# One unrolled pipeline through all heads of the first two attentions, key-major values for two groups, the block quantisation at other steps, and SiLU as one ScalarE function

## The reference

```python
x = x + tanh(g_xattn[i]) * attention_i(layernorm(x), ctx)
x = x + tanh(g_ffn[i])   * ffn_i(layernorm(x))
```

```python
q = latents @ Wq; k, v = hidden_states @ Wk, hidden_states @ Wv   # hidden_states = context, then latents
out = softmax(q k^T * scale) v                                    # 8 (or 4) heads share one k and one v
return out @ Wo
```

## Time and profile before

| | us |
|---|---|
| median of 3 runs | 1492.81 (1490.13 to 1494.4) |
| the profiled execution: its own time | 1491.04 |
| its span, first to last instruction | 1489.3 |
| PE busy | 1369.5 (92%) |
| DVE busy | 965.4 (65%) |
| ACT busy | 599.4 (40%) |
| POOL busy | 467.3 (31%) |
| attention 0, about | 44 to 654 |
| attention 1, about | 729 to 1062 |
| network of layer 2, about | 1284 to 1398 |
| network of layer 3, about | 1417 to 1487 |

### The profile page before, as it was taken

The page is one execution under the profiler, slowest core; times in us unless marked ns, Lnnn a source line. Parts: engine busy times, 40 slices in busy tenths (PEclk is TensorE's granted clock), DMA queues, the critical chain, the costliest instruction groups (busy, mean ns, idle before and its releaser), DMA issues.

```text
span 1489.3 us, 22423 instructions
## 1 busy us (share of the span) xinstructions
PE 1369.5 (92%) x8021; PEld 1073.0 (72%) x8027; DVE 965.4 (65%) x1394; ACT 599.4 (40%) x1037; POOL 467.3 (31%) x357
## 2 busy tenths in 40 slices
PE   5999989998999999989899999999689999899765
PEld 4898879887889888854687887878665444577422
DVE  3778657874878478853584865746655773463697
ACT  2544434443444344420443534434325677122111
POOL 2361445153434334421242243530232002144100
PEclk9999999999999999999999999999888999999878
DMA  5210112011110211021002011110230000561000
GB/s 184 57 40 22 61 45 61 28 61 44 36 47 22 68 57 47 8 78 37 27 1 65 21 53 32 32 38 9 72 96 1 1 2 1 139 163 44 0 0 29
DMA packets 54335, 68.13 MB, mean 46 GB/s; under 512 B 26416, under 2 KB 34896, under 8 KB 54240
## 3 DMA queue, kind: packets, MB, share of 16 engines
q1 hardware_dynamic: 54240, 66.84, 14.9%
HBM read 57.13 MB, written 5.37 MB: 42 GB/s over the span
## 4 chain that ended last, share of the span: by engine, by line
PE 80%; DVE 12%; issue 3%; ACT 3%; DMA 1%; POOL 0%; SPq 0%; DVEq 0%; POOLq 0%; ACTq 0%
PE ps L637 12%; PE ps L611 11%; PE ps L549 9%; PE ps L625 9%; PE ps L576 8%; PE ps L569 8%; PE ps L1502 4%; PE ps L1133 3%; PE ps L1159 3%; PE ps L1515 2%; DVE pT L824 2%; PE ps L1115 1%; ACT pT L715 1%; PE ps L1144 1%; PE ps L882 1%
## 5 line engine op out<-in xcount | busy, mean ns | idle before, releaser
L715 ACT ACTIVATE pT<-ps 128x768 fp32r<-128x768 f32 x192 | 156.0, 812 | 291.8 <-PE ps L625 291.8
L637 PE MATMUL ps<-pT,vv 128*128 128x256 f32 (+1 forms) x1728 | 249.7, 289 | 2.5 <-DVE oT L830 2.5
L824 DVE TENSOR_TENSOR pT<-ps,pT 128x768 fp32r<-128x768 f32 x192 | 183.7, 957 | 92.9 <-ACT pT L715 92.5
L611 PE MATMUL ps<-kT,qT 128*128 128x512 f32 (+3 forms) x1152 | 233.0, 339 | 4.0 <-DVE qT L767 2.6
L611 PEld LDWEIGHTS ps<-kT,qT 128*128 128x128 f32 (+1 forms) x1152 | 198.9, 188 | 43.5 <-DVE qT L767 4.2
L637 PEld LDWEIGHTS ps<-pT,vv 128*128 128x128 f32 (+1 forms) x1728 | 215.5, 180 | 4.3 <-DVE pT L824 2.9
L813 DVE TENSOR_REDUCE nmax<-ps 128x1 f32<-128x768 f32 x192 | 182.2, 951 | 23.0 <-PE ps L611 20.1
L722 ACT ACTIVATE prob<-ps,nmax 128x768 f32<-128x768 f32 x192 | 172.2, 897 | 30.2 <-DVE nmax L813 30.0
L625 PE MATMUL ps<-ident,prob 128*128 128x128 f32 x1152 | 158.7, 274 | 19.2 <-DVE pT L824 19.2
L576 PE MATMUL ps<-wo,oT 128*128 128x512 f32 (+1 forms) x576 | 163.5, 399 | 4.3 <-DVE qT L767 2.6
L625 PEld LDWEIGHTS ps<-ident,prob 128*128 128x128 f32 x1152 | 130.8, 140 | 31.6 <-ACT prob L722 17.8
(11 more groups left out here) (224 smaller groups left out, 1869.2 us busy)
## 6 DMA issues: line engine op xcount, KB each, us to landing
f2raw<-in_f_w SPq DMA_DIRECT2D x11, 776.0 KB, 4.5
w3in<-in_m_w SPq DMA_DIRECT2D x11, 768.0 KB, 4.5
raw<-in_l_wq SPq DMA_DIRECT2D x32, 256.0 KB, 2.8
raw<-in_l_wo SPq DMA_DIRECT2D x32, 256.0 KB, 2.6
raw<-in_l_wq SPq DMA_DIRECT2D x16, 192.0 KB, 2.4
raw<-in_l_wo SPq DMA_DIRECT2D x16, 192.0 KB, 2.4
w3gu<-w3o SPq DMA_DIRECT2D x11, 256.0 KB, 2.6
ctxraw<-in_ctxT SPq DMA_DIRECT2D x2, 1024.0 KB, 7.6
```

The costliest lines, as they stand in the source:

```text
L611: last = nc.tensor.matmul(sc[:, lo:hi], qT[0:hd, h % 2, qp, r * P:(r + 1) * P], kT[0:hd, kp, b, lo:hi], start=(qp, kp) == PAIRS[0], stop=( ...
L637: last = nc.tensor.matmul(bank(6, 256, hd), vv[:, vp, b * VT + j, 0:hd], pT[:, q % 2, pp, j, :], start=(j == 0 and (vp, pp) == PAIRS[0]), ...
L715: nc.scalar.activation(turned_p(m, HI), ps[:, 4:6, 0:S // 2].rearrange("p a (j c) -> p a j c", j=3), ACT.Copy).then_inc(s["pT_hi"], 1)
L824: nc.vector.tensor_tensor(to, ps[:, 4:6, 0:S // 2].rearrange("p a (j c) -> p a j c", j=3), hi, ALU.subtract).then_inc(s["pT"], 1)
```

## The change

Four things are changed together.

1. **One pipeline.** Both attentions run one pipeline through all heads (128 and 64 items), without loop and without draining between groups. The K jobs of the next group are jobs on bank 7 in the steps around the change of group, and the four O jobs in banks of their own remain only as two at the very end.
2. **Values key-major.** V is projected with the keys as weights and the value weights of two groups moving: 6 jobs V of 24 matmuls with 256 columns (192 in attention 1) for two groups, on bank 7, in steps 0 to 4 and again at the start of group 2. The transposes are gone.
3. **The w3 blocks at other steps.** The tiles start at heads 1, 4, 9, 12, 17, 20, 25, 28 of attention 0 and 1, 5, 9 of attention 1; the three blocks of a tile stand in steps 4h+2, 4h+6 and 4h+10, so where n mod 4 = 2. Their buffers now lie over `xn` and `xTf`.
4. **SiLU on ACT.** ACT's function Silu takes the place of tanh and of the first DVE multiplication. In the layer 3 network the scale of a block is multiplied from `amax` itself (a factor of 16 goes into `gate16`), and the last hidden row is quantised in two parts. PE no longer waits for `layer_done` before attention 3.

The core of the diff:

```diff
+        for h in range(heads):
+            n = RT * h
+            if h + 1 < heads:
+                last[n + 1] = ("Q", h + 1, 0)
+            last[n + 6], last[n + 7], last[n + 8], inner[n + 9] = [("O", h, r) for r in range(RT)]
+        for u in range(1, kv):
+            n = RT * self.g * u
+            inner[n - 2], inner[n - 1], inner[n] = ("K", u, 0), ("K", u, 2), ("K", u, 1)
...
+                inner[n + 2], last[n + 2], inner[n + 3], inner[n + 4], last[n + 4], inner[n + 5] = v
...
+        for i, h in enumerate(tiles):
+            n = first_tile + i
+            self.amax_at[RT * h + 2], self.scale_at[RT * h + 6], self.step_at[RT * h + 10] = n, n, n
...
+                elif kind == "V":
+                    wait("split", A.split["v", h, 1])
+                    batch, j = divmod(c, 3)
+                    for i in range(2):
+                        for k in range(KT):
+                            for xp, wp in PAIRS:
...
+                                last = nc.tensor.matmul(ps[:, b, i * 2 * hd:(i + 1) * 2 * hd], keys,
+                                                        wv[:, wp, k * 2 * hd:(k + 1) * 2 * hd],
...
+            def job_in_turn(what):
+
+                wait("w", A.place[what] - 1)
+                job(what, 7)
...
+            for n, inner, end in A.steps:
+                if n < A.items:
+                    scores(n)
+                if inner:
+                    job_in_turn(inner)
+                if 2 <= n < A.items + 2:
+                    turn(n - 2)
+                if n >= 4:
+                    weighted(n - 4)
+                if end:
+                    job_in_turn(end)
...
-                    if n % RT == 1 and A.quantises(it):
-                        if n // RT in A.amax_at:
-                            block_maxima(A.tile(it, A.amax_at[n // RT]))
...
+                if n in A.amax_at:
+                    block_maxima(A.amax_at[n])
+                if n in A.scale_at:
+                    scale_weights(A.scale_at[n])
+                if n in A.step_at:
+                    step_of_weights(A.step_at[n])
+                if end:
+                    job(end, 7)
...
-                nc.scalar.activation(fe[:], bank(4), ACT.Tanh, scale=0.5).then_inc(sem("f2_e"), 1)
+                nc.scalar.activation(fe[:], bank(4), ACT.Silu).then_inc(sem("f2_e"), 1)
...
-                nc.scalar.activation(me[:], flat(0), ACT.Tanh, scale=0.5).then_inc(sem("m3_e"), 1)
+                nc.scalar.activation(me[:], flat(0), ACT.Silu, scale=16.0).then_inc(sem("m3_e"), 1)
...
-                nc.vector.scalar_tensor_tensor(me[:], me[:], 1.0, flat(0), ALU.add,
-                                               ALU.mult).then_inc(sem("m3_g"), 1)
-                v.wait_ge(sem("m3_g"), r + 1)
                 v.wait_ge(sem("m3_up"), r + 1)
-                nc.vector.scalar_tensor_tensor(mh[:], me[:], 0.5, flat(3), ALU.mult,
+                nc.vector.scalar_tensor_tensor(mh[:], me[:], 16.0, flat(3), ALU.mult,
```

More of the change, by code:

```diff
@@ L103, in __init__ @@
[L103 to L128, removed]
+        assert len(self.place) == len(order) == 3 * kv + 3 * kv + heads + RT * heads
+        self.hi_place = {j: i + 1 for i, j in enumerate(j for j in order if j[0] != "O")}
+        need = [(RT * h - 3, 0, ("q", h, 0)) for h in range(heads)] + [(RT * h + 6, 1, ("o", h, 0)) for h in range(heads)]
@@ L131, in build @@
+        count.update({n: self.items for n in ("scores", "nmax", "exps", "turned", "pT_hi", "pT")})
+        count.update({n: self.pairs for n in ("pv", "oT_hi", "oT")})
+        self.before = before.after if before else dict.fromkeys(count, 0)
+        self.after = {n: self.before[n] + count[n] for n in count}
+A0 = Attention("l0", 32, 4, 128, (1, 4, 9, 12, 17, 20, 25, 28), 0, None)
+A1 = Attention("l1", 16, 4, 96, (1, 5, 9), 8, A0)
+TAIL_BANK = {2: 3, 3: 6}
 def build(nc, t, out):
@@ L432, in att_total, with att_wait @@
[L432 to L450 removed]
+        def att_wait(engine, A, name, n):
+            if A.before[name] + n > 0:
+                engine.wait_ge(sem(f"att_{name}"), A.before[name] + n)
@@ L664, in att_pe @@
-            values(0)
-            with pe.Fori(0, A.kv - 1) as it:
-                head(it, True)
-            head(A.kv - 1, False)
-        def kv_dst(A, part, c):
+            job(A.first[2], 2)
+            job(A.first[3], 7)
+            for n, inner, end in A.steps:
[9 more added lines that the diff above has]
+                    job_in_turn(end)
@@ new lines, in att_act @@
+            for n, inner, end in A.steps:
+                early = inner and inner[0] != "O"
+                if early:
+                    if n < A.items:
+                        exponentials(n)
+                    job(inner, 7)
+                if 2 <= n < A.items + 2:
+                    turned(n - 2)
+                if not early and n < A.items:
+                    exponentials(n)
+                if n >= 5 and n % 2 == 1:
+                    q = (n - 5) // 2
+                    h, b = divmod(q, B)
+                    wait("pv", q + 1)
+                    nc.scalar.activation(oT[0:hd, h % 2, HI, b * 256:(b + 1) * 256], bank(6, 256, hd),
+                                         ACT.Copy).then_inc(sem("att_oT_hi"), 1)
+                if end:
+                    job(end, 7)
@@ L859, in mlp0_early_sp @@
+            s = 1 if A is A0 else 3
+            v.wait_ge(sem("w3_done"), 4 * A.stored)
+            for r in range(RT):
+                what = ("O", A.heads - 1, r)
+                if what in A.tail:
+                    job(what, TAIL_BANK[r])
+                ln_row_dve(v, s, r, sem("att_w"), A.before["w"] + A.place[what])
         def mlp0_early_sp(sp):
```

709 lines of the change are left out of this document (319 added, 390 removed).

## The result

| | before | changed |
|---|---|---|
| median, same chip (us) | 1490.13 (1483.42 to 1494.4) | 1498.73 (1498.1 to 1501.35) |
| the profiled execution's own time | 1491.04 | 1501.35 |
| PE busy | 1369.5 | 1382.1 |
| DVE busy | 965.4 | 937.0 |

The ratio is 1.0066, with a 95% interval from 1.0034 to 1.0097: slower, by 0.7%. The medians differ by 8.6 us and the profiled executions by 10.3; I had forecast 14.3 for the latter.

The account below looks back on a forecast made before the run. PE was taken to bound the kernel, with DVE having slack on average. Attention 0 +17.3, attention 1 +2.0 and the layer 3 network -5 gave +14.3 us on 1491.04, so 1505, range 1482 to 1521.

Parts of the forecast that it names:

- part 3: w3 blocks ahead of row tile 0's addition delay PE: 3.3 us a tile, 32.7 us more over 11 tiles.
- the three places: Head with a block of maxima: row tile 1 late by 0.7 us, weighted sum by 0.3, row tile 3 by 0.3.
- The sign that I gave: O jobs waiting for DVE's addition by about 0.7 us and more, once in each w3 block.
- the four that I had named: Four of attention 0's 8 tiles, three heads after the last, disturbed by POOL's splits: 0.2 us added on the mean.
- My threshold of 1.7: Block length in us from which a w3 block ahead of the addition was to decide; all three blocks are longer.
- Part 1: Values projected key-major without transposes: 2.4 us less in attention 0, 7.9 less in attention 1.
- Part 2: One pipeline, drains gone but jobs waiting at bank 7: 3.1 us less in attention 0, equal in attention 1.
- Part 4: Silu on ACT removes a DVE operation: about 5 us less in the layer 3 network, nothing in layer 2.
- The blocks are absorbed: Rival: PE's queued work covers the w3 blocks at the new steps too, giving 1479 us, faster; chance 0.23.
- The blocks are disturbed: Rival: POOL's splits fall beside every block of maxima, 1.6 us more each, giving 1523 us; chance 0.08.
- The change of group gives more: Rival: jobs at bank 7 hardly wait, another 13 us less, giving 1492 us, no change; chance 0.07.

Follow-up runs that it names:

- Experiment 3: The changed kernel with the w3 blocks in the same steps but behind the addition of row tile 0 instead of ahead of it: 1500.32 us, ratio 1.0059.
- experiment 1: The changed kernel with the three w3 blocks one step earlier, at 4h+1, 4h+5 and 4h+9: 1469.18 us, ratio 0.9852 to the kernel before.
- experiment 5: The changed kernel with tanh and the second DVE multiplication back in the layer 3 network alone: 1510.79 us, ratio 1.0141 to the kernel before.
- experiment 7: Changed kernel with blocks one step earlier, three V jobs on bank 6, two-input small operations, last row's addition between the quantisation parts: 1458.66 us, ratio 0.9786.

## Why the prediction was nearly right

I forecast 1505, slower; it is 1498.73, slower. What decides is part 3, as forecast, and the sizes of several terms were off in opposite directions. That the total came so near is partly luck: attention 0 came out 5.3 below its forecast and attention 1 8.0 above, and the stretches before and behind attention 1, which I had put at nothing, gave 6.2.

**Part 3.** Right in the three places and in the heads without a block, too large in price. The sign that I gave, an O job waiting 0.7 and more for the addition in each block, came only in part: the blocks of maxima show it, with 0.21 in the first, the scaling and the step blocks don't. A tile costs 0.93 + 0.43 + 0.71 = 2.1 where the small operations are short, and 2.9 where one is held; I had 1.4 + 0.7 + 1.1 and 0.2 for the held ones, which is 3.4 and not the 3.3 that I went on with. The held ones are four tiles of attention 0, the four that I had named; they cost 0.85 more each. And one block of maxima in each attention stands at the start of group 2, where O jobs follow behind the V jobs: it costs 3.1 (23.43 from Q to Q against 20.28 in experiment 1, and 23.17 against 20.09), a place that I hadn't looked at. Against experiment 1, and with the 2.3 that its own blocks cost, the 8 tiles of attention 0 come to 21.8, not 26.4. In the first block I had row tile 1 late by 0.7 and it was 0.37, the weighted sum by 0.3 and it was 0.29, row tile 3 by 0.3 and it was 0.11. The block lasts 2.20 (78.49 to 80.69), not 2.4, and the addition's result reaches PE 0.79 after it began, not 0.9. Experiment 3 shows the deeper fault in the picture: inside a head the price isn't the addition's delay but DVE's lag. My threshold of 1.7 is too high as well: by it the scaling, at 1.75, would cost next to nothing, and it costs 0.43. In attention 1, measured the same way, it is 12.3 against 9.9, as step blocks met the K jobs (1.85 each), which I had overlooked too.

**Part 1.** The values in attention 1 are the term that was sized wrong: 288 matmuls at 0.115 are 33.1, so 5.0 less and not 7.9. I drew a slope through 512 and 256 columns and carried it on below 256, where the measured matmuls hardly get cheaper: 0.111 for 192 columns with no wait before them, 0.115 behind a wait. With 256 columns I had been too high (0.128, measured 0.120; and 288 of them at 0.128 are 36.9, so 2.5 less and not 2.4). The Trainium skill, "TensorE: Matmul & The Clock Gate", section "Back-to-back issue gap", has N/2.4 + 2.5 ns for an isolated matmul, 42.5 ns for 96 columns and 82.5 for 192, and says itself that this under-counts a stream with weight loads at small N. The traces, with 113 and 115, agree with that warning. That the formula would have led me near 1499 is chance: by it the values of attention 1 would have given 14.3, an estimate from the formula, and they gave 5.0.

**Part 2.** Values and waits together gave 6.2 less in attention 0 (12.0 against the 18.2 of the blocks, 21.8 minus 3.6), I had 5.5. At 0.120 a matmul about 4.8 of it are the values, where I had 2.4, so only about 1.4 are waits, where I had 3.1. From start to start the waits are the ones of the forecast: 1.58 for 1.65 (35.55 - 31.18 - 2.79), 0.68 for 0.6 (41.31 - 39.58 - 1.05), 1.15 for 1.1 (50.50 - 48.77 - 0.58). What I left out is the 0.1 by which the piece behind each is longer.

**The clock.** In attention 1, two K jobs took 4.59 instead of 3.0 at a lower clock (0.66 from 724 to 729), 3.2 of that stage's 10.0. The blocks with 12.3, the values with -5.0 and this give 10.5, so that stage is accounted for. The kernel before had one such stretch elsewhere (5.29 instead of 3.60 at 659.00, granted clock 0.74 from 660 to 665), most of the -2.5 between the two attentions. The -3.7 between attention 1 and layer 3 is of this kind as far as I can tell: that work is almost unchanged, and two kernels with the same code there, the changed one and that of experiment 1, took 356.3 and 359.6. Why the clock differs is open.

**Part 4.** -5.5 for the stage, -5 predicted; experiment 5 gives 5.75 for the operation and its consequences. Silu takes 1.34 on 128x1408 as tanh does in experiment 5. The rows are 11.7 and 12.0 apart, not 12.4. Before the last transposes PE waits 4.94 for the addition that stands behind both parts; experiment 7 took 1.4 of it, of which 1.0 reached the multiplication behind.

**The rivals.** "The blocks are absorbed" was wrong here and comes true one step earlier: 1469. "The blocks are disturbed" holds for 4 of the 11 tiles in this execution, at 0.85 each. "The change of group gives more" is out.

## What to carry over

Side work on an engine with slack on average still has to stand where its consumer has something long to do: here, right behind the start of a 2.8 us job, and not one step later, which cost 26 to 32 us. Price such a move by the lag that it leaves the engine with in that stretch, not by the one result that it delays; and look at every place where the block falls, the changes of group too. Don't carry a price beyond the sizes that the trace shows: ask for bounds there.

## What the runs showed of the hardware

- fp32r matmuls in runs of 12 or 24, each with a weight load: 0.113 us for 96 columns and 0.115 for 192 behind a wait, 0.111 for 192 without one, 0.120 for 256 (0.122 behind a wait), 0.2325 for 512.
- A DVE operation on 128x48 takes 0.19 us, but one that begins beside a POOL split lasts until the split has ended: 0.99 beside one of 1.04 with two inputs, and 1.03 beside one of 1.04 with one. The Trainium skill, "SBUF — State Buffer", section "SBUF: two separate sides", has the two engines share a port pair under an exclusive lock, and names the DVE operations that take it: those in a two-port performance mode, and those with two SBUF inputs against a POOL operation that reads SBUF. The small operations with two inputs agree. The reduction that kept its 1.75 has one input, so it doesn't speak against the lock; in which mode it and the small operations with one input run, no trace here shows.
- With fewer columns in six jobs a stretch of 38.45 us was 8.3 longer, the granted clock being 0.63 and 0.67 in parts of it: the clock can cost more than a smaller job gives. That the fewer columns caused it isn't shown.
